# Two expert layers around attention on one core: token transposes ahead of their waits, layer-norm moments between the router's mask steps, the token table written in halves

## The chip, the cores and the metric

One core of one Trainium2 chip runs the whole program. The metric is the device time of one execution in microseconds. TensorE does matrix products and transposes, VectorE, ScalarE and GpSimd (POOL in the views) do the elementwise work, SyncE (SP) issues most DMAs. Each engine runs its own instructions in order; semaphores tie them together.

## The reference

The input x is 8 x 256 tokens of 256 numbers, fp32. Three residual layers follow each other:

```python
x = x + 0.5 * ffn(layernorm(x), router_w, w1, v1, w2)
x = x + attention(layernorm(x), Wq, bq, Wk, bk, Wv, bv, Wo, bo)
x = x + 0.5 * ffn(layernorm(x), router_w, w1, v1, w2)
```

`ffn` is a mixture of 64 experts of width 96. The eight highest of softmax(x @ router_w.T) are a token's experts, their weights are scaled to sum 1, an expert takes its first 32 tokens in an order that goes over the tokens, computes silu(x w1) * (x v1) and multiplies by w2; the weighted results are added back to the tokens. Attention has 16 heads of 128 in 4 groups that share keys and values, over 8 sequences of 256.

## The kernel before, in words

Tokens lie in 16 tiles of 128. Both expert layers run through the same helpers, named `expert_layer(layer)` on each engine, with attention between them.

**Router.** A pair of tiles is transposed on TensorE (`transpose_tokens`, L1178) and copied by ScalarE (`copy_tokens`, L556). `experts_of(n)` multiplies four tiles by the router's weights (L1188), ScalarE copies (L560), `logits_of(n)` transposes back (L1199), ScalarE copies to `logits` (L564). VectorE has a mask step for each four tiles: MAX8 (L822), MATCH_REPLACE8 of the eight highest (L826), and `chosen` by comparison (L828). GpSimd subtracts the maximum (L486), multiplies by 1/sigma (L490), ScalarE takes the exponential (L600), GpSimd multiplies by the mask (L494). The layer norm's statistics are BATCH_NORM_STATS2 (L742 at the start, L1020 behind attention), its moments a chain of small operations on VectorE (`moment_steps`, 11 levels at L755; `shifts`, L785). In layer 0 all 16 tiles go in one chain ahead of the masks; in layer 1 it is 12 tiles, and then the last four once attention has given them.

**Slots.** From `chosen` TensorE makes codes (L1226), VectorE finds each expert's tokens (L835 to L862, `slot_index`), ScalarE normalises the tokens (L574), and SP writes tokens (`store_tokens`, L379) and weights (`store_weights`, L385) to a table in HBM. When slots are known and the table is whole, GpSimd gathers 128 rows of it for each of 16 groups of four experts (L506). TensorE is kept busy with filler products meanwhile (`keep_busy`, L1121).

**Experts.** `slot_step(s)` of each engine handles one group: transpose of the slots (L1084), products with `up` (L1152), silu (L543) and product (L809), transpose (L1145) and copy (`hiddenT`, L539), products with `down` (L1162), and later the sums into tokens (L1113, L1097).

**Loads.** SP issues everything in one order. A group's weights are `up` (768 KB) and `down` (512 KB), into one of 12 homes named q, r, o, s. SP issues groups 0 to 3, the table, groups 4 to 11, then 12 to 15 as homes become free, with wk behind 12 and wv behind 13, wq and wo at the end. In layer 1 groups 0 to 3 are issued within attention, 4 to 7 at `attention_done`, then the table, and the others after the first two gathers.

**Attention weights.** fp32 values are split in a high and a low part: `split_high` on ScalarE (L622), `split_low` on VectorE (L931), in the order of the list `splits`. Four early ones stand in slot steps 11 to 15, the others in attention. `project` on TensorE waits until K_SPLIT, V_SPLIT or Q_SPLIT of them are done. `first_fills` is the order of the first projections: xT, xT, k, q, q, v, v, q, q; `in_fill` says behind which of them VectorE does a split.

## Time and profile before

| what | value |
|---|---|
| median of 3 runs | 687.88 us (687.8 to 689.42) |
| profiled execution, its own time | 689.65 us |
| its span, first to last instruction | 687.9 us |
| mean granted TensorE clock | 0.964 |
| TensorE busy | 630.9 us (92%) |
| VectorE busy | 504.6 us (73%) |
| ScalarE busy | 390.5 us (57%) |
| GpSimd busy | 50.8 us (7%) |

Times in the rows are from the start of the span. PE is TensorE, DVE is VectorE, ACT is ScalarE, SPq the queue in which SP issues DMAs, PEclk the granted clock as a share of 2.4 GHz. In a row `[2.25 <-DVE wq_lo L931]` says that the engine stood idle for 2.25 us before it and what ended that. A group such as "4.03 ACT L574 ... x8" is eight instructions that took 4.03 us from first start to last end.

### The profile page before, as it was taken

How to read it: one execution, taken by the hardware profiler on the slowest of the kernel's cores; microseconds unless marked ns; L12 is line 12 of the kernel's file. 1: busy time of each engine (PE TensorE's matmuls, PEld its weight loads, DVE VectorE, ACT ScalarE, POOL GpSimd, SP SyncE). 2: the span in 40 equal slices, each digit the busy share in tenths (PEclk: the TensorE clock that was granted, in tenths of full speed). 3: DMA queues.
4: the chain of work that ended last, by engine and by line, in shares of the span. 5: the costliest groups of instructions: out<-in, count | busy, mean ns of one | idle time of the engine just before them, and what ended most of it. 6: DMA issues, size and time to landing. Idle time of an engine off the chain costs nothing.

```text
span 687.9 us, 12266 instructions
## 1 busy us (share of the span) xinstructions
PE 630.9 (92%) x4626; PEld 542.3 (79%) x4626; DVE 504.6 (73%) x1312; ACT 390.5 (57%) x1051; POOL 50.8 (7%) x68
## 2 busy tenths in 40 slices
PE   8489887999999999999999999999999999947995
PEld 6267665899898979999897999989799998625774
DVE  5846656689997777778777777877777787684663
ACT  4724454567666565666655566665556666572341
POOL 2343000000000000000000000000000000034310
PEclk9779998899999999999999999999999999978998
DMA  9799960000000000000000000000000007196971
GB/s 316 259 386 403 373 221 1 0 1 1 1 2 1 1 0 1 1 1 1 1 1 1 1 0 1 1 1 1 1 1 1 1 7 301 70 369 242 344 271 49
DMA packets 27135, 62.53 MB, mean 91 GB/s; under 512 B 6880, under 2 KB 17120, under 8 KB 26816
## 3 DMA queue, kind: packets, MB, share of 16 engines
q1 hardware_dynamic: 25008, 55.92, 22.1%
q0 software_dynamic: 1632, 5.38, 2.2%
q8 instruction: 39, 0.64, 0.4%
q10 hardware_dynamic: 432, 0.39, 0.2%
q14 instruction: 24, 0.20, 0.1%
HBM read 54.34 MB, written 7.34 MB: 90 GB/s over the span
## 4 chain that ended last, share of the span: by engine, by line
PE 77%; DVE 9%; ACT 5%; DMA 3%; another core or an unknown queue 2%; issue 1%; POOL 1%; SPq 1%; DVEq 0%; POOLq 0%; ACTq 0%
PE bank L1291 19%; PE bank L1293 18%; PE bank L1292 18%; PE bank L1345 8%; PE bank L1113 3%; PE bank L1152 3%; DMA down_r<-down_in 3%; PE bank L1162 2%; PE bank L1084 1%; PE bank L1097 1%; PE bank L1266 1%; DMA slots<-token_table,slot_index 1%; DVE ln L755 1%; DVE o_lo L983 1%
## 5 line engine op out<-in xcount | busy, mean ns | idle before, releaser
L664 ACT ACTIVATE probs<-bank,negmax 128x256 f32<-128x256 f32 x256 | 121.5, 494 | 0.0
L677 ACT CAST probsT_hi<-bank 128x512 fp32r<-128x512 f32 x128 | 68.9, 590 | 82.3 <-PE bank L1345 82.3
L997 DVE TENSOR_REDUCE negmax<-bank 128x2 f32<-128x512 f32 x128 | 82.0, 681 | 2.3 <-PE bank L1293 2.3
L1029 DVE TENSOR_TENSOR probsT_lo<-bank,probsT_hi 128x512 fp32r<-128x512 f32 x128 | 82.0, 682 | 1.4 <-ACT probsT_hi L677 1.4
L647 ACT ACTIVATE o_hi<-bank,bv 128x512 fp32r<-128x512 f32 x64 | 44.2, 690 | 64.5 <-PE bank L1293 64.5
L1291 PE MATMUL bank<-k_hi,q_hi 128*128 128x256 f32 x256 | 73.2, 286 | 2.9 <-DVE q_lo L983 2.9
L1005 DVE TENSOR_SCALAR probs<-probs,rowinv 128x256 f32<-128x256 f32 x256 | 73.1, 350 | 2.3
L983 DVE SCALAR_TENSOR_TENSOR o_lo<-bank,bv,o_hi 128x512 fp32r<-128x512 f32 x64 | 48.0, 750 | 36.0 <-ACT o_hi L647 35.8
L1291 PE MATMUL bank<-o_hi,wo_hi 128*128 128x256 f32 x256 | 72.9, 285 | 0.7 <-DVE o_lo L983 0.7
L1293 PE MATMUL bank<-k_hi,q_lo 128*128 128x256 f32 x256 | 73.0, 285 | 0.0
L1292 PE MATMUL bank<-k_lo,q_hi 128*128 128x256 f32 x256 | 72.9, 285 | 0.0
L1293 PE MATMUL bank<-o_hi,wo_lo 128*128 128x256 f32 x256 | 72.3, 282 | 0.0
L1292 PE MATMUL bank<-o_lo,wo_hi 128*128 128x256 f32 x256 | 72.1, 282 | 0.0
L983 DVE SCALAR_TENSOR_TENSOR q_lo<-bank,bq,q_hi 128x512 fp32r<-128x512 f32 x64 | 48.0, 749 | 31.3 <-ACT q_hi L647 31.2
L1345 PE MATMUL bank<-ident,probs 128*128 128x128 f32 x512 | 67.2, 275 | 0.6 <-DVE probs L1005 0.6
L1345 PEld LDWEIGHTS bank<-ident,probs 128*128 128x128 f32 x512 | 58.2, 142 | 1.1 <-DVE probs L1005 1.1
L664 ACT ACTIVATION_READ_ACCUMULATOR probs<-bank,negmax 128x1 f32 x256 | 57.7, 225 | 0.0
L1291 PE MATMUL bank<-xT_hi,wq_hi 128*128 128x512 f32 x128 | 55.1, 430 | 2.3 <-DVE wq_lo L931 2.3
L1291 PE MATMUL bank<-probsT_hi,v_hi 128*128 128x512 f32 x128 | 51.4, 401 | 4.0 <-DVE xT_lo L981 3.2
L647 ACT ACTIVATE q_hi<-bank,bq 128x512 fp32r<-128x512 f32 x64 | 45.0, 702 | 17.1 <-PE bank L1293 17.1
L1291 PEld LDWEIGHTS bank<-k_hi,q_hi 128*128 128x128 f32 x256 | 49.4, 193 | 6.1 <-DVE q_lo L983 3.7
L1292 PEld LDWEIGHTS bank<-k_lo,q_hi 128*128 128x128 f32 x256 | 49.4, 193 | 2.3
(178 smaller groups left out, 1347.9 us busy)
## 6 DMA issues: line engine op xcount, KB each, us to landing
up_r<-up_in SPq DMA_DIRECT2D x16, 768.0 KB
down_r<-down_in SPq DMA_DIRECT2D x14, 512.0 KB
up_q<-up_in SPq DMA_DIRECT2D x8, 768.0 KB, 9.1
up_o<-up_in SPq DMA_DIRECT2D x6, 768.0 KB
down_q<-down_in SPq DMA_DIRECT2D x8, 512.0 KB, 10.1
token_table<-xn SPq DMA_DIRECT2D x16, 256.0 KB, 2.8
down_o<-down_in SPq DMA_DIRECT2D x6, 512.0 KB
x<-x_in SPq DMA_DIRECT2D x4, 512.0 KB, 5.6
```

The costliest lines, as they stand in the source:

```text
L647: nc.scalar.activation(dst, src, ACT.Identity, bias=bias).then_inc(work_high, 1)
L664: nc.scalar.activation(probs[:, n % 2, t, :], scores_ps[head][:, qt * S:qt * S + S], ACT.Exp, bias=negmax[:, n % 2, t:t + 1], accum_out=ro ...
L677: nc.scalar.copy(probsT[0][:, head].rearrange("p c s -> p (c s)"), probsT_ps[head][:]).then_inc(probsT_high, 1)
L983: nc.vector.scalar_tensor_tensor(lo, src, bias, hi.bitcast(f32), ALU.add, ALU.subtract).then_inc(work_taken, 1)
L997: nc.vector.reduce_max(negmax[:, n % 2, 2 * head:2 * head + 2], scores_ps[head][:].rearrange("p (t s) -> p t s", t=2), AX.X, negate=True). ...
L1005: last = nc.vector.tensor_scalar(probs[:, n % 2, t, :], probs[:, n % 2, t, :], rowinv[:, n % 2, t:t + 1], None, ALU.mult)
L1029: nc.vector.tensor_tensor(probsT[1][:, head].rearrange("p c s -> p (c s)"), probsT_ps[head][:], probsT[0][:, head].rearrange("p c s -> p ( ...
L1113: last = mm(banks[n][:, D * pair:D * pair + D], marks[:, c:c + P], parts, start=start and pair == 0, stop=stop, skip_group_check=True)
L1291: mm(dst, w[0], m[0], start=start, stop=False, skip_group_check=shared)
L1292: mm(dst, w[0], m[1], start=False, stop=False, skip_group_check=shared)
L1293: return mm(dst, w[1], m[0], start=False, stop=stop, skip_group_check=shared)
L1345: last = nc.tensor.transpose(probsT_ps[head][:, c * S + qt * P:c * S + qt * P + P], probs[:, n % 2, 2 * head + qt, c * P:c * P + P], ident[:])
```

## The change

- **Start.** 5 instead of 14 filler products. The first four tiles are transposed before the wait for the centred router weights, with other orders of transposes, expert products and logits in both layers; logits go through banks 2 and 3 instead of 6 and 7.
- **Moments.** A new `masks(layer, n, between)` on VectorE runs moment levels between its own operations. In layer 0 masks 0 and 1 hold all 11 levels. In layer 1 mask 0 with the levels of the first 12 tiles is done before the last output, and the moments of the last four tiles are on GpSimd (`last_moments`, 21 operations).
- **End of attention.** Tokens 0 and 1 of layer 1 are transposed in attention's last step; expert product 0, transposes 2 and 3 and logits 0 go before its last output product, expert product 1 and transposes 4 and 5 before its output transposes. `attention_done` is given before the last statistics.
- **Table.** GpSimd waits for all masks before it multiplies, then multiplies in two halves; exponentials and weights go in halves too. ScalarE normalises 12 tiles, takes the exponentials, then 4. SP writes tokens 0 to 2, weights 0, tokens 3, weights 1.
- **Loads.** Three groups instead of four before the table in layer 0, and two instead of four between `attention_done` and the table in layer 1. wk, the first quarter of wq, wv, the rest of wq and wo follow behind all groups.
- **Splits.** The first two of wq come before those of wv; all four early ones move out of steps 11 to 15 to the end of the first expert layer.

```diff
-            for g in range(4):
+            for g in range(3):
                 load(0, g)
-            for n in range(4):
-                store_tokens(n)
-            store_weights()
-            for g in range(4, AHEAD):
+            store_table()
+            for g in range(3, AHEAD):
                 load(0, g)
...
+            sp.dma_start(wq_raw[:, :, 0:G * DH], by_column[:, :, 0:G * DH]).then_inc(wq_first_loaded, 16)
...
-            for g in range(len(homes_q), 8):
+            for g in range(len(homes_q), 6):
                 load(1, g)
...
-        K_SPLIT, V_SPLIT, Q_SPLIT, O_SPLIT = 2, 4, [6, 8, 12, 16], [10, 14, 18, 20]
+        K_SPLIT, V_SPLIT, Q_SPLIT, O_SPLIT = 2, 6, [4, 8, 12, 16], [10, 14, 18, 20]
...
+            def store_table():
+                for n in range(3):
+                    store_tokens(n)
+                store_weights(0)
+                store_tokens(3)
+                store_weights(1)
...
+            def last_moments():
...
+                pool.wait_ge(last_stats, 1)
+                tt(half_gap, stats[:, a:b, 1], stats[:, a:b, 4], ALU.subtract)
+                tt(mean_, stats[:, a:b, 1], stats[:, a:b, 4], ALU.add)
+                tie(tt(var, stats[:, a:b, 2], stats[:, a:b, 5], ALU.add))
...
+                tie(tt(var, var, gap2, ALU.add))
+                tie(ts(rstd_.bitcast(i32), var.bitcast(i32), -0.5, ROOT_BITS, ALU.mult, ALU.add))
...
                 pool.wait_ge(shifted, shift_seen.add(4))
+                pool.wait_ge(chosen_ready, masks.add(4))
                 pool.wait_ge(moments_ready, 2 * layer + 1)
-                nc.gpsimd.tensor_tensor(expw[:], expw[:], rstd.unsqueeze(2).to_broadcast([P, TILES, E]),
-                                        ALU.mult).then_inc(scaled_ready, 1)
+                for h in range(2):
+                    tiles = slice(8 * h, 8 * h + 8)
+                    nc.gpsimd.tensor_tensor(expw[:, tiles, :], expw[:, tiles, :], rstd[:, tiles].unsqueeze(2).to_broadcast([P, 8, E]),
+                                            ALU.mult).then_inc(scaled_ready, 1)
...
+                if layer == 0 and s == GROUPS - 1:
+                    split_high(0)
...
-                normalise(0, TILES // 2)
+                normalise(0, TILES - 4)
...
             expert_layer(0)
+            for n in range(2, 5):
+                split_high(n)
...
+            def masks(layer, n, between=()):
...
+                for a in range(4 * n, 4 * n + 4):
+                    top = nc.vector.max(top8[:, a, :], logits[:, a, :])
+                    if a == 4 * n + 3:
+                        top.then_inc(top8_ready, 1)
+                    chore()
...
-            moments(0, TILES)
+            steps = moment_steps(0, TILES)
+            masks(0, 0, steps[:7])
+            masks(0, 1, steps[7:])
             shifts(0, TILES)
+            masks(0, 2)
+            masks(0, 3)
...
-            in_fill = {1: 4, 2: 5, 3: 6, 4: 7, 6: 8, 7: 9}
+            in_fill = {1: 3, 2: 4, 3: 5, 4: 6, 6: 7, 7: 8, 8: 9}
...
-            moments(0, TILES - 4)
+            masks(1, 0, moment_steps(0, TILES - 4))
             shifts(0, TILES - 4)
-            last = output(BLOCKS - 1)
-            nc.vector.sem_inc(attention_done, 1)
-            tie(last)
-            moments(TILES - 4, TILES)
-            shifts(TILES - 4, TILES)
+            output(BLOCKS - 1).then_inc(last_stats, 1)
+            for n in range(1, 4):
+                masks(1, n)
             expert_layer(1)
...
-            for _ in range(14):
+            for _ in range(5):
                 mm(bank[3][:, 0:P], ones, ones, start=True, stop=True)
...
-            for u in range(2):
-                transpose_tokens(1, u)
-            output_product(STEPS - 1)
             experts_of(1, 0)
             transpose_tokens(1, 2)
+            transpose_tokens(1, 3)
+            logits_of(1, 0)
+            output_product(STEPS - 1)
+            experts_of(1, 1)
+            transpose_tokens(1, 4)
+            transpose_tokens(1, 5)
             output()
             expert_layer(1)
```

## Rows read from the trace of the kernel before

**Rows 1.** Busy time by stage: us, busy (instructions) of each engine, clock, DMA, GB/s.
```profile
8.00:26.00 18.00, 10.99 (x78) 7.17 (x79) 16.66 (x85) 11.76 (x25) 4.39 (x5) 0.95 0.95 359
45.00:94.00 49.00, 44.91 (x562) 31.57 (x551) 31.03 (x116) 22.03 (x68) 9.65 (x11) 0.97 1.03 386
128.00:590.00 462.00, 453.54 (x2960) 408.83 (x2959) 368.82 (x786) 289.32 (x798) 0.00 (x0) 1.00 0.03 12
```

**Rows 2.** The chain that ended last, first router: start us, us, what.
```profile
15.30 0.19 DVE ln L755
20.14 0.53 DVE top L822 x4
...
21.59 0.42 DVE chosen L828
23.47 2.03 DVE chosen L828
```

**Rows 3.** Instructions in order of time, 1 to 26 us; x's landing; a small iota.
```profile
1.07 6.34 PE L1266 MATMUL bank<-xnT 128*128 128x128 f32 x28 [1.07 <-DVE xnT L726]
8.12 5.32 DVE L742 BATCH_NORM_STATS2 stats<-x 128x6 f32<-128x256 f32 x16
8.30 1.06 PE L1178 MATMUL bank<-ident,x 128*128 128x128 f32 x8 [0.49 <-issue]
22.61 0.62 POOL L486 TENSOR_TENSOR expw<-logits,top 128x256 f32<-128x256 f32 x1 [1.26 <-DVE top L822]
23.31 1.90 POOL L490 TENSOR_TENSOR expw<-expw,ln 128x1024 f32<-128x1024 f32 x1
...
DMA to landing us min/median/max: 4.1/5.6/7.3
...
L462 POOL IOTA part_offset<- 64x4 int32 x2 | 0.3, 131 | 0.1
```

**Rows 4.** Instructions in order of time, 20 to 33 us, ScalarE and SP's queue.
```profile
20.20 4.04 ACT L574 ACTIVATE xn<-x,ln 128x256 f32<-128x256 f32 x8
...
32.61 0.91 SPq L370 DMA_DIRECT2D up_r<-up_in  x1
```

**Rows 5.** End of the first expert stage: ScalarE in order of time, then the chain.
```profile
74.60 0.63 ACT L622 ACTIVATE wk_hi<-wk_raw 128x512 fp32r<-128x512 f32 x1 [2.90 <-DMA wk_raw<-wk_in]
...
69.98 17.71 DMA down_r<-down_in
```

**Rows 6.** Landing of wo; TensorE in order of time; the chain there.
```profile
DMA to landing us min/median/max: 21.8/21.8/21.8
...
105.66 0.47 PE L1291 MATMUL bank<-xT_hi,wq_hi 128*128 128x512 f32 x1 [2.25 <-DVE wq_lo L931]
...
107.60 0.43 PE bank L1293
```

**Rows 7.** TensorE, the last output product, in order of time.
```profile
592.28 0.39 PE L1291 MATMUL bank<-o_hi,wo_hi 128*128 128x256 f32 x1 [0.69 <-DVE o_lo L983]
```

**Rows 8.** The second router, in order of time.
```profile
596.06 1.28 DVE L1014 TENSOR_TENSOR x<-x,bank 128x512 f32<-128x512 f32 x2 [1.15 <-PE bank L1371]
608.90 2.02 DVE L828 TENSOR_TENSOR chosen<-struck,logits 128x256 fp32r<-128x256 f32 x1
611.64 4.04 ACT L574 ACTIVATE xn<-x,ln 128x256 f32<-128x256 f32 x8
```

**Rows 9.** From slots to the experts of layer 1, in order of time.
```profile
621.58 5.51 PE L1121 MATMUL bank<-router_w,ident 128*128 128x128 f32 x32
622.24 1.00 POOL L506 DMA_INDIRECT slots<-token_table,slot_index  x1 [8.07 <-DVE slot_index L862]
625.21 0.22 DVE L794 TENSOR_REDUCE total<-slots 128x1 f32<-128x64 f32 x1 [2.83 <-DMA slots<-token_table,slot_index]
629.30 0.37 ACT L605 COPY slotsT<-bank 128x256 f32<-128x256 f32 x1 [12.11 <-remote]
630.09 0.86 PE L1152 MATMUL bank<-up_q,slotsT 128*32 128x192 f32 x16
```

More of the change, by code:

```diff
@@ L483, in expert_layer @@
                 for n in range(4):
+                    if layer == 1 and n == 1:
+                        last_moments()
                     pool.wait_ge(top8_ready, tops.add())
@@ L534, in slot_step @@
                                    bank[0][:, 0:KD * P]).then_inc(slotsT_ready, 1)
-                if layer == 0 and SPLIT_AT <= s < SPLIT_AT + SPLIT_EARLY:
-                    split_high(s - SPLIT_AT)
                 if s > 0:
@@ L540, in slot_step @@
                                    bank[2][0:F, 0:P]).then_inc(hiddenT_ready, 1)
+                if layer == 0 and s == GROUPS:
+                    split_high(1)
                 if s < GROUPS:
@@ L679, in step @@
                 jobs = fills(n, last)
+                if last and n == STEPS - 1:
+                    copy_tokens(0)
+                    copy_tokens(1)
                 for head in range(2):
@@ L810, in slot_step @@
                                             ALU.mult).then_inc(hidden_ready, 1)
+                if layer == 0 and s == GROUPS:
+                    split_low(0)
+                    split_low(1)
                 if s > 0:
@@ L1381, in step @@
                 jobs = fills(n, last)
+                if last and n == STEPS - 1:
+                    for u in range(2):
+                        transpose_tokens(1, u)
                 for m, job in enumerate(jobs):
```

192 lines of the change are left out of this document (118 added, 74 removed).

## The prediction

> **What bounds the kernel now.** I read the busy time by stage first [rows 1]. From 128 to 590 us TensorE is busy 453.5 of 462 us at full clock: that is attention, and the change leaves it alone. The rest, some 225 us, is two expert layers with a router ahead of each. In 8 to 26 us VectorE is the busy one (16.7 of 18 us), and layer 1's router is built like this one; in 45 to 94 us the DMA engines never rest (share 1.03, 386 GB/s); between routers and experts runs a chain of short steps.
>
> The second view is the chain that ended last. In the first router it is VectorE without a break: the moments, then four mask steps of 1.88 us each (from the maxima at 20.14 to the end of `chosen` at 22.01), and the last mask's final operation takes 2.03 us instead of 0.42 [rows 2]. It starts 0.16 us after a GpSimd multiply of 1.90 us and ends 0.3 us after it [rows 3]: two engines in each other's way, 1.6 us lost. The same stands in layer 1 (2.02 us at 608.90) [rows 8].
>
> Third, the SP queue. It issues four loads, then stands until tokens and weights of the table are ready, since its order has them first, and issues the next load only at 32.61 [rows 4]. All later loads hang on that time, and the chain of the first expert stage ends on the load of the last group, which lands at 87.69 us [rows 5].
>
> **Sum for layer 0.** Today 14 first matmuls (28 records) run from 1.07 to 7.41, 0.226 us each, and column sums, centring and only then the statistics (8.12) follow [rows 3]. With 5 of them TensorE is through at 3.4. The x pieces are issued from 1.23 to about 2.8 and take 4.1 to 7.3 us, so they land from 5.3 to 10.1 [rows 3]. The last four statistics (0.33 us each) end at 11.4 instead of 13.44: 2.0 us gained.
>
> The clock takes part of it back. 0.226 us for a record is half clock (1.2 GHz); the same 128-column transposes take 0.13 us at full clock, after 6 us of activity [rows 3]. The 9 matmuls taken away were that activity. The new first token transposes start at 5.3, probably at half clock. Two pairs of transposes, one expert product and one transpose of logits, 1.1 + 0.6 + 1.1 + 0.4 us and copies at full clock, take some 7 us at half: logits 0 are there at about 12.3, logits 1 at about 15.8. VectorE then does a mask (1.88) and seven moment levels. A level alone costs 0.20 us [rows 2]; between maxima I take 0.15, since the wait for its predecessor is filled. The GpSimd subtraction of 0.62 us runs at that time and can block the levels that read two tiles, as it blocked the mask [rows 3]; I take 0.3 us (0 to 0.6). So masks 0 and 1 with all moments end at 18.3, the shift at 18.5, masks 2 and 3 at 22.3, against 25.50: 3.2 us, of which 1.6 is the collision, since the multiply now waits for the last mask.
>
> ScalarE begins to normalise at 18.6 instead of 20.20. Twelve tiles at 0.505 us (4.04 for 8) reach 24.6, two half exponentials 25.7, four tiles 27.7 [rows 4]. SP issues tokens 3 and the second half of the weights by 30.0. The loads resume there instead of 32.61. But only three loads were issued ahead instead of four. From 32.61 to 87.69 twelve groups and wk and wv (0.8 of a group) landed, 4.3 us for one [rows 4 and 5]. Now thirteen groups come first, and the attention weights behind: 30.0 + 13 x 4.3 = 85.9 instead of 87.69. **Gain 1.8 us**, and its point of no gain is a restart at 31.8. The gathers go off 3.4 us sooner, but that is hidden by these loads. The wait of ScalarE for wk at 74.6 (2.90 us idle) goes [rows 5], but the load takes its place.
>
> Behind the last group wk, the first quarter of wq and wv must land at about +1.5, +3.0 and +4.5 us after it. ScalarE asks for them, in order, at +1.9, +4.1 and +5.3 us (its positions in steps 15 and 16); behind the first of these waits stands its copy of hiddenT, for which TensorE waits. Priced at nothing, at most 1.5 us. ScalarE has one split between the copies of x and its table load now, where it had two: **0.5 us**. wo, issued at 76.5, took 21.8 us to 98.3 [rows 6] and comes 0.6 us after ScalarE wants it; k_hi is 2.6 us away, so nothing.
>
> **Head of attention.** TensorE waits 2.25 us for wq_lo, because q needs six splits and VectorE does the last behind k; then it runs at half clock (0.43 us start to start for 512 columns instead of 0.23) for ten matmuls [rows 6]. With q ahead of wv in the order of splits q needs four, done in the fill before. I follow the fills with that: scores start 6.7 us after xT instead of 10.1. v now needs split 6 and costs a bit. I take **3.0 us**, ends 1.0 and 4.0 (the wait alone less the new one for v, or all of the half clock as well).
>
> **Layer 1.** Tokens 0 and 1 are transposed (1.03 us) ahead of an output product, so the last attention product comes 0.85 us later. TensorE then does an expert product, two pairs of transposes and a transpose of logits before the last output product, 2.5 us where 1.0 us of work and 0.69 of waiting stood [rows 7]. Output of x is done at about 599.45 instead of 597.34: 2.1 us later. Mask 0 with 11 levels of moments (about 3.9 us) lies ahead of it on VectorE, from 594.05, and ends about when y comes; its old cover was idle time. After it VectorE has 1.4 us of statistics and three masks without moments: 600.85 + 3 x 1.88 + 0.3 us of blocking = 606.8 against 610.92 [rows 8]. Everything up to the slots follows, and the 16 filler products start at 617.5 instead of 621.58. They take 5.5 us to 623.0, and the first gather (3.0 us from issue to VectorE's first use) lands at 621.2, so they stay last [rows 9]. **4.1 us.**
>
> The table must keep up. Counting row times through the new order, ScalarE has its last logits at 603.6, the identity copies till 604.5, 12 tiles till 610.6, exponentials till 611.7, the last tiles till 613.7 (615.68 now); weights issued by 615.4 land at about 618, when slots are ready too [rows 8]. GpSimd: attention_done at 599.5, two operations, one subtraction, 601.0; then 21 small operations, 17 of them in a chain. The trace has none like these there. Lower bound: 0.131 us (a 4-element iota) with 0.08 between, 4.4 us. Upper: 0.62 (a 256-element one), 15 us. The two tensor_tensor sizes, 0.62 for 256 and 1.90 for 1024 elements, give 0.19 plus 1.67 ns for each element [rows 3]; I take 0.20 and 0.12 us between: 6.0 us, to 607.0. Three subtractions, two multiplies: 611.0, and ScalarE comes to the exponentials at 610.6. So 0.3 us is lost, hidden by 0.7 us of slack ahead of SP's turn.
>
> The Trainium skill, "GPSIMD Engine Reference", section 4.1, says the opposite of the change: elementwise work belongs on VectorE, GpSimd being about twice as slow with two inputs. Rows here give 0.62 against 0.42 us for 256 elements. By its factor on the 2.75 us of moments the sum would be 5.5 us and no other.
>
> Loads: two groups instead of four ahead of the table, so it meets less traffic; groups 6 to 11 then start at about 623. Group 6 is wanted 16 us after the start of the experts, group 11 32 us; at 4.3 us a group they are in time.
>
> Between the end of the fillers (627.1) and ScalarE's copy of slot 0 (629.30, released by "remote") lie 0.2 us for two transposes and some 2.0 us for which the trace names nothing [rows 9]. I can't say whether they stay: half of it, **1.0 us** (0 to 2).
>
> Sum: 1.8 + 0.5 + 3.0 + 4.1 + 1.0 = 10.4 us. The profiled execution took 689.65 us around a span of 687.9, so 679.2; the median of the three runs is 687.88, so **677.5 us**.
>
> **Rivals.**
> (a) *The loads eat layer 0.* If the restart is later than 31.8, one group fewer ahead costs up to 4.3 - 2.6 us. For: half clock in the first router. With no gain there and 1.5 us of waits for wk: 677.5 + 1.8 + 1.5 = 680.8. Chance 0.17.
> (b) *The new wait takes the gain of layer 1.* GpSimd's chain at 0.4 us an operation plus gaps is 10.5 us: the end of the table slips 4 us, and with it the gathers: 681.5. Chance 0.10.
> (c) *Slower than before.* The same chain at 1.00 us each, the time of this engine's gather instruction [rows 9]: 22 us with less between, gathers 16 us later than in my sum less 0.7 of slack, 692.8. It passes the time of before from about 0.72 us an operation. Against: every arithmetic row of this engine lies on the line above. Chance 0.03.
> (d) *It doesn't do what it says*: TensorE's early work only delays the end of attention and logits come as late as before, the layer 1 part is nil: 682.6. Against: three of four masks need no late logits. Chance 0.06.
> (e) *All covers hold*: clock up early, full 4.0 at the head, 2.0 us gone: 687.88 - (3.4 + 0.5 + 4.0 + 4.1 + 2.0) = 673.9. Chance 0.14.
> Forecast, 675 to 680: 0.50.
>
> Range 672.5 to 683: it takes in (a), (b), (d) and (e). About 0.3% (2 us) is what a measurement of this kernel can tell. Faster by more: 0.92; within 0.03; slower 0.05 ((c), and part of what I haven't seen).
>
> **What would show it.** Layer 0: statistics end near 11.4; the last chosen is 0.42 us long and ends near 22.3; first up_r issue near 30 and last load near 86; no wait at TensorE for wq_lo. Layer 1: x added 2 us later, last chosen near 607, GpSimd's chain about 6 us, no long wait of a gather for the table, experts 5 us sooner. Wrong if the half clock reaches past 12 us, if GpSimd's operations are far above 0.2 us, or if the waits for wk, wq or wv stop ScalarE at the end of the first expert stage.

## The result and the profile after

| what | before | after |
|---|---|---|
| median beside each other | 688.1 us (687.8 to 689.42, 4 runs) | 678.81 us (677.92 to 681.17, 4 runs) |
| profiled execution, its span | 689.65, 687.9 us | 678.44, 676.7 us |
| mean granted clock | 0.964 | 0.973 |
| from the start to the addition of x in layer 1 | 596.06 | 590.16 |
| from there to the first `up` of layer 1 | 34.03 | 27.88 |
| from there to the end of the span | 57.8 | 58.66 |

The changed kernel takes 0.9867 of the time before (95% interval 0.9838 to 0.9895); a second series gave 0.9865 (0.9842 to 0.9888). The difference is 9.3 us between medians and 11.2 us between the spans of the two profiled runs: that of before lies 1.55 us above its median, that of after 0.37 below. The last three lines of the table split the 11.2 us: 5.9 and 6.15 gained, 0.85 lost.

Line numbers are new: the moments are L813, `chosen` L896, `best_rank` L913, `part_bits` L915, the gather L544, `up` L1228, the fillers L1197. The same stretches as in [rows 1], with the same columns:

```profile
8.00:26.00 18.00, 14.38 (x86) 8.44 (x84) 15.78 (x88) 14.11 (x31) 6.12 (x8) 0.81 0.87 321
45.00:94.00 49.00, 43.68 (x523) 32.43 (x517) 29.94 (x116) 22.87 (x65) 8.47 (x9) 0.97 1.03 385
128.00:590.00 462.00, 453.65 (x2982) 409.07 (x2981) 367.18 (x803) 290.38 (x799) 0.00 (x0) 1.00 0.03 12
```

TensorE is busy for 14.38 of the 18 us at clock 0.81, where it was for 10.99 at 0.95; 3.68 us of the 14.38 are products on tokens that came behind 26 us before. VectorE is no longer the one that never rests there (15.78 against 16.66). The loads run at 385 GB/s as before, and attention is the same.

The first router of after, answering to [rows 2, 3], in order of time (start us, length us, engine, line, operation, and in brackets the idle time before it):

```profile
9.98 1.40 DVE L800 BATCH_NORM_STATS2 stats<-x 128x6 f32<-128x256 f32 x4 [0.32 <-DMA x<-x_in]
...
12.66 0.62 POOL L522 TENSOR_TENSOR expw<-logits,top 128x256 f32<-128x256 f32 x1 [6.71 <-DVE top L886]
...
12.81 0.50 DVE L813 TENSOR_TENSOR ln<-ln 128x16 f32<-128x16 f32 x1
...
20.09 0.43 DVE L896 TENSOR_TENSOR chosen<-struck,logits 128x256 fp32r<-128x256 f32 x1
...
24.41 2.49 POOL L533 TENSOR_TENSOR expw<-expw,chosen 128x512 f32<-128x512 f32 x2 [1.71 <-ACT expw L652]
...
26.12 0.82 DVE L913 CAST best_rank<-best 128x32 int32<-128x32 f32 x1
```

The statistics end at 11.38, and what ends VectorE's wait is the landing of x. One level of moments takes 0.50 us instead of 0.16, and a subtraction of GpSimd runs beside it. The last `chosen` takes 0.43 us, where it took 2.03 [rows 2]. But `best_rank`, 0.18 us long in other runs, takes 0.82 beside the mask multiplication, which now comes at that time.

Loads and the head of attention in after, answering to [rows 4 to 6]:

```profile
28.95 0.57 SPq L371 DMA_DIRECT2D up_q<-up_in  x1
...
83.32 1.15 PE L1228 MATMUL bank<-up_r,slotsT 128*32 128x192 f32 x16 [2.27 <-DMA down_r<-down_in]
...
104.46 0.47 PE L1375 MATMUL bank<-wv_hi,xT_hi 128*128 128x512 f32 x1 [0.40 <-DVE wv_lo L1003]
...
105.91 0.28 PE L1375 MATMUL bank<-k_hi,q_hi 128*128 128x256 f32 x1
...
118.41 0.47 PE L1375 MATMUL bank<-xT_hi,wk_hi 128*128 128x512 f32 x1
```

SP issues loads again at 28.95 (32.61 before), and the load of the last group ends TensorE's wait at 83.27 (87.69). The wait of 2.25 us for wq_lo is gone; one of 0.40 us for wv_lo stands in its place. The scores start at 105.91.

The second router of after, answering to [rows 8]:

```profile
590.16 1.28 DVE L1090 TENSOR_TENSOR x<-x,bank 128x512 f32<-128x512 f32 x2
...
592.97 0.20 POOL L488 TENSOR_TENSOR ln<-stats 128x4 f32<-128x4 f32 x1 [0.86 <-DVE stats L1098]
...
598.09 0.42 DVE L896 TENSOR_TENSOR chosen<-struck,logits 128x256 fp32r<-128x256 f32 x1
...
598.20 0.37 POOL L506 TENSOR_TENSOR ln<-ln 128x4 f32<-128x4 f32 x1
...
598.94 0.23 POOL L508 TENSOR_SCALAR ln<-ln 128x4 f32<-128x4 f32 x1
...
603.25 2.52 POOL L533 TENSOR_TENSOR expw<-expw,chosen 128x512 f32<-128x512 f32 x2 [0.21 <-ACT expw L652]
...
603.68 0.88 DVE L913 CAST best_rank<-best 128x32 int32<-128x32 f32 x1
...
604.68 1.24 DVE L915 TENSOR_TENSOR part_bits<-best_code,bit_of_part 128x128 int32<-128x128 int32 x1
```

GpSimd's chain runs from 592.97 to 599.17. The last `chosen` ends at 598.51 and is short. Again the collision has moved: `best_rank` takes 0.88 and `part_bits` 1.24 us beside the two mask multiplications (2.52 us), 1.65 us more than the 0.18 and 0.29 that they take where nothing runs beside them. It works the other way round too: of GpSimd's 21 small operations three take 0.35 to 0.37 us where their like take 0.20, and each of the three begins within a `chosen` of VectorE and ends 0.05 to 0.07 us after it (the row at 598.20).

From the slots to the experts of layer 1, answering to [rows 9]:

```profile
610.38 6.61 PE L1197 MATMUL bank<-router_w,ident 128*128 128x128 f32 x32
...
611.05 1.07 POOL L544 DMA_INDIRECT slots<-token_table,slot_index  x1 [5.28 <-DVE slot_index L933]
...
616.58 0.94 POOL L544 DMA_INDIRECT slots<-token_table,slot_index  x1 [0.30 <-issue]
...
618.04 0.86 PE L1228 MATMUL bank<-up_q,slotsT 128*32 128x192 f32 x16
...
623.56 0.41 PE L1160 MATMUL bank<-ident,slots 128*128 128x128 f32 x2 [0.56 <-DMA slots<-token_table,slot_index]
```

The fillers take 6.61 us (5.51 before). The gather issued at 616.58 lands at 623.4, 6.8 us later, and TensorE waits 0.56 us for it.

### The profile page after: what moved, and what is told of

It reads as the page before. It is cut to its first block, busy times and chain, and to the rows that moved or that the text cites. A ratio compares the mean times of both kernels' runs of the same rounds, so it can differ in the third digit from the quotient of the medians.

```text
span 676.7 us, 12242 instructions
## 1 busy us (share of the span) xinstructions
PE 625.8 (92%) x4608; PEld 538.1 (80%) x4608; DVE 500.7 (74%) x1297; ACT 390.5 (58%) x1053; POOL 56.1 (8%) x93
## 3 DMA queue, kind: packets, MB, share of 16 engines
q0 software_dynamic: 1632, 5.38, 2.2%
## 4 chain that ended last, share of the span: by engine, by line
PE 74%; DVE 11%; DMA 7%; ACT 3%; issue 2%; POOL 1%; SPq 0%; DVEq 0%; ACTq 0%; POOLq 0%
PE bank L1375 19%; PE bank L1377 18%; PE bank L1376 18%; PE bank L1429 8%; PE bank L1189 3%; DMA down_r<-down_in 3%; DMA slots<-token_table,slot_index 3%; PE bank L1228 2%; PE bank L1238 1%; PE bank L1173 1%; DMA x<-x_in 1%; DVE struck L892 1%; PE bank L1160 1%; DVE ln L813 1%; ACT probs L717 1%
## 5 line engine op out<-in xcount | busy, mean ns | idle before, releaser
L700 ACT ACTIVATE o_hi<-bank,bv 128x512 fp32r<-128x512 f32 x64 | 44.2, 690 | 63.7 <-PE bank L1377 63.7
## 6 DMA issues: line engine op xcount, KB each, us to landing
up_r<-up_in SPq DMA_DIRECT2D x16, 768.0 KB, 12.3
```

The costliest lines, as they stand in the source:

```text
L700: nc.scalar.activation(dst, src, ACT.Identity, bias=bias).then_inc(work_high, 1)
```

## Experiments

Each is compared with the kernel before on the same chip; run N below is the one under number N. The changed kernel itself, in its second series, is the measure for the small differences (an "x us more" is between its median and the run's). Runs 1 to 3 stood beside it on one chip; 4 to 7 were taken on a second chip, 8, 9 and 11 on a third, 10 in a later series on the first. The kernel before had 688.13, 688.16, 687.14 and 687.25 us in these four series, so a difference across them is uncertain by about 1 us, and the ratios to the kernel before are the better measure:

> The changed kernel itself, so that the experiments beside it have it on the same chip. It had 0.9867 of the kernel before (0.9838 to 0.9895). Expected: the same within 0.3%, about 679 us where the kernel before has 688; last chosen of layer 0 at 20.5 us of the span, first up of layer 1 at 618.0. If the first comparison had owed part of its 9.3 us to the chip, the ratio would come out above 0.99.

Measured: 679.35 us (677.09 to 681.18, 6 runs), 0.9865. Its rows repeat the first trace: last `chosen` at 20.54, `up` of layer 1 at 618.56. From the start of x's addition to that `up` it has 27.92 us (27.88). Single runs of one kernel spread over 4 us, so below the rows decide wherever medians lie within 2 us.

**1. Moments back on VectorE.**

```diff
-                    if layer == 1 and n == 1:
-                        last_moments()
...
-            output(BLOCKS - 1).then_inc(last_stats, 1)
+            tie(output(BLOCKS - 1))
+            moments(TILES - 4, TILES)
+            shifts(TILES - 4, TILES)
```

> The moments of the last four tiles of layer 1 go back from GpSimd to VectorE; all else is the changed kernel. Theory (VectorE is the path in layer 1's router, from the x addition to the last chosen): its 24 small instructions return to a chain that costs about 0.13 us for each, 24 x 0.13 = 3.1 us, so the last chosen ends about 3 us later than at 598.5 and the kernel takes about 681.7 us (+2.9). Rival (the slot fillers and the first gather set the start of layer 1's experts, and VectorE's last chosen has slack): within 0.5 us of the changed kernel. A second rival, GpSimd's chain was itself late at the end (last level 599.2 after a last chosen that ended at 598.5): then taking it away costs only about 2 us.

Measured: 681.28 us, 0.9892 (0.9874 to 0.991), 1.9 us more. VectorE in order of time:

```profile
608.46 0.18 DVE L911 CAST best_rank<-best 128x32 int32<-128x32 f32 x1
...
608.75 0.29 DVE L913 TENSOR_TENSOR part_bits<-best_code,bit_of_part 128x128 int32<-128x128 int32 x1
```

The last `chosen` ends 11.1 us after x's addition started, 8.35 in the changed kernel: 2.7 us, as the theory says. But the masks come later than GpSimd's multiplications (604.99 to 607.50) now, `best_rank` and `part_bits` are back at 0.18 and 0.29, and 1.2 us come back: `up` starts 29.11 us after x's addition, against 27.88. Moving the moments brought 2.7 us on VectorE and gave 1.2 back in a collision of its own making (and 0.3 in fillers that ran longer at half clock). Between medians the part is not clear of the spread: the intervals of the two ratios overlap.

**2. v before q.**

```diff
+            sp.dma_start(wv_raw[:], wv_in.rearrange("(k p) n -> p k n", p=P)).then_inc(wv_loaded, 16)
             sp.dma_start(wq_raw[:, :, 0:G * DH], by_column[:, :, 0:G * DH]).then_inc(wq_first_loaded, 16)
-            sp.dma_start(wv_raw[:], wv_in.rearrange("(k p) n -> p k n", p=P)).then_inc(wv_loaded, 16)
...
-        K_SPLIT, V_SPLIT, Q_SPLIT, O_SPLIT = 2, 6, [4, 8, 12, 16], [10, 14, 18, 20]
+        K_SPLIT, V_SPLIT, Q_SPLIT, O_SPLIT = 2, 4, [6, 8, 12, 16], [10, 14, 18, 20]
...
-            in_fill = {1: 3, 2: 4, 3: 5, 4: 6, 6: 7, 7: 8, 8: 9}
+            in_fill = {1: 4, 2: 5, 3: 6, 4: 7, 6: 8, 7: 9}
```

> The head of layer 0's attention back as it was: v's weights are loaded and split before the first q's, with the places of the split in the order of the projections moved back; all else is the changed kernel. Theory: of the changed kernel's gain, 3.3 us (loads to last slot transposes to scores) and 1.3 us (second and third projections at full instead of half clock) came from q being computed before v, so this takes 3.3 to 4.6 us more than the changed kernel, about 682.5 us, and VectorE's low half of the first q's weights is again what the tensor engine waits for near 103 us. Rival: the head follows the loads of the last expert group alone, and the order of q and v moves nothing; within 0.5 us of the changed kernel.

Measured: 680.75 us, 0.9896 (0.9867 to 0.9925), 1.4 us more.

```profile
103.87 0.47 PE L1376 MATMUL bank<-xT_hi,wq_hi 128*128 128x512 f32 x1 [2.25 <-DVE wq_lo L1003]
...
117.29 0.39 PE L1376 MATMUL bank<-k_hi,q_hi 128*128 128x256 f32 x1 [2.68 <-DVE q_lo L1059]
```

The wait for wq_lo is back to the hundredth. From the last wait for weights (83.95) to the second block's first scores (117.29) it takes 33.3 us; 31.3 and 31.5 in the two traces of the changed kernel. The order is worth 1.9 us here, not the 3.3 to 4.6 expected. The rest of what the head gained is clock, which can fall either way: these scores run at full clock (0.39 us), those of the changed kernel at half (0.58). So at a later landmark, the second block's first product for v, little of the 1.9 us is left: it comes 38.92 us after the last wait, 38.34 and 38.63 in the two traces of the changed kernel.

**3. Fourteen fillers.**

```diff
-            for _ in range(5):
+            for _ in range(14):
```

> Fourteen pairs of filler products ahead of layer 0's router instead of five; all else is the changed kernel. Theory (the early router is on the path to the restart of the weight loads): the logits start about 2 us later than at 11.0 us if the fillers hold the tensor engine, the last chosen of layer 0 ends about 1.5 to 2 us later than at 20.5, the loads restart so much later than at 28.95, and the kernel takes about 680.6 us (+1.8). Rival 1 (the landing of x at 10.0 us holds the statistics whatever the tensor engine does, and the fillers end before it): within 0.3 us. Rival 2 (the fillers bring the clock up earlier): the logits at full clock, 0.5 us faster.

Measured: 680.08 us, 0.9883 (0.9862 to 0.9904), 0.7 us more, which is inside the spread. The statistics wait for the centred weights again and run from 7.12 to 12.43, so the last `chosen` of layer 0 ends at 21.54, 1.0 us later, yet the loads restart at 29.09 against 28.95. Five traces of other kernels whose code is the changed kernel's up to there (its second series, runs 1, 2, 4 and 5) restart them at 28.02 to 29.90. Taking the fillers away gave VectorE 1 us and the loads nothing that can be measured.

**4. Four groups ahead of the table in layer 1**, as before the change:

```diff
-            for g in range(len(homes_q), 6):
+            for g in range(len(homes_q), 8):
...
-            for g in range(6, AHEAD):
+            for g in range(8, AHEAD):
```

> Four expert groups of weights instead of two are issued ahead of the table's stores in layer 1, as in the kernel before; all else is the changed kernel. Theory (the loads of layer 1 compete with the gathers: the gather issued at 616.6 took 6.8 us while loads that were issued from 615.4 ran): with two groups loaded earlier the gathers meet fewer loads, and the wait of 0.56 us and the late hidden near 620 go, 0.3 to 1.0 us less. Rival (the table stands behind the two groups on its queue, 2 groups by some 4 us): the table is stored later, the first gather lands later than 614.07 and, beyond 3 us, the experts of layer 1 start later; 0 to 3 us slower.

Measured: 683.53 us, 0.9942 (0.9921 to 0.9963), 4.2 us more. GpSimd and TensorE:

```profile
614.37 1.07 POOL L544 DMA_INDIRECT slots<-token_table,slot_index  x1 [9.60 <-issue]
...
617.46 0.44 PE L1160 MATMUL bank<-ident,slots 128*128 128x128 f32 x2 [1.44 <-DMA slots<-token_table,slot_index]
```

The first gather starts at 614.37, though x was added 1.0 us sooner than in the changed kernel, whose gather starts at 611.05. Its wait is not ended by slot_index but by the table ("issue": no event of an engine). The stores of tokens into the table take 7.2 us to land in the median (2.4 in the changed kernel, 4.5 in the kernel before). So the rival holds. The edit of two numbers, which I had priced at nothing, is worth 4.2 of the 9.3 us (5.3 us by the ratios, whose intervals lie apart).

**5. Eight fillers in layer 1.**

```diff
-                keep_busy(16)
+                keep_busy(8 if layer == 1 else 16)
```

> Eight pairs of filler products instead of sixteen between slot keys and slot transposes of layer 1; all else is the changed kernel. Theory (in the changed kernel the fillers end at 617.0, 2.9 us after the first gather landed at 614.07, so that they and not the gather set the start of layer 1's experts): they end near 613.7, the first slot transposes start at the gather's landing, near 614.1 instead of 616.8, and the kernel takes 1 to 2.7 us less, about 677 us; less where fewer fillers leave the clock low at the start of the experts. Rival (the weights of the first groups or slotsT hold the experts anyway): within 0.5 us of 679.35, the changed kernel's median beside the first experiments.

Measured: 680.85 us, 0.9892 (0.9873 to 0.9911), 1.5 us more.

```profile
617.16 0.86 PE L1228 MATMUL bank<-up_q,slotsT 128*32 128x192 f32 x16
...
622.88 0.66 PE L1160 MATMUL bank<-ident,slots 128*128 128x128 f32 x2 [2.67 <-DMA slots<-token_table,slot_index]
...
623.68 1.51 PE L1228 MATMUL bank<-up_q,slotsT 128*32 128x192 f32 x16
```

The experts do start 2.3 us sooner after x's addition (25.58 against 27.88). Then TensorE waits 2.67 us for the third group's tokens, and the next `up` takes 1.51 us instead of 0.86: half clock. From that `up` to the end it takes 63.7 us instead of 58.7. The gain that was expected is not there: the next limit is the gathers. The 1.5 us between medians are not clear of the spread.

**6. Masks in pieces.**

```diff
-                    nc.gpsimd.tensor_tensor(expw[:, 8 * h:8 * h + 8, :], expw[:, 8 * h:8 * h + 8, :],
-                                            chosen[:, :, h, :].bitcast(f32), ALU.mult).then_inc(weights_ready, 1)
+                    for part in range(4):
+                        a = 8 * h + 2 * part
+                        last = nc.gpsimd.tensor_tensor(expw[:, a:a + 2, :], expw[:, a:a + 2, :],
+                                                       chosen[:, 2 * part:2 * part + 2, h, :].bitcast(f32), ALU.mult)
+                    last.then_inc(weights_ready, 1)
```

> GpSimd's multiplication of the exponentials by the masks, two instructions of 2.5 us in each layer, is issued in four pieces each; all else is the changed kernel. Theory (VectorE's instructions wait while a GpSimd instruction runs, so best_rank takes 0.88 instead of 0.18 and part_bits 1.24 instead of 0.29 in layer 1, 1.65 us together, and best_rank 0.82 in layer 0): a blocked instruction waits for one piece of about 0.7 us at most, so part_bits takes under 0.9 us, the slot keys of layer 1 are ready 0.3 to 1.0 us sooner after the last chosen (11.6 us in the changed kernel), and the kernel takes 0.3 to 1.0 us less, or nothing less if the fillers behind the slot keys take it up. Rival (the time goes with the bytes both engines move, not with the length of GpSimd's instruction): the two instructions are as long as before. Cost: 6 more GpSimd instructions per layer, by 0.1 to 0.2 us, and the table up to 1 us later.

Measured: 680.71 us, 0.9892 (0.9873 to 0.9911), 1.4 us more.

```profile
605.66 0.48 DVE L916 CAST best_rank<-best 128x32 int32<-128x32 f32 x1
...
606.26 0.43 DVE L918 TENSOR_TENSOR part_bits<-best_code,bit_of_part 128x128 int32<-128x128 int32 x1
...
605.23 3.57 POOL L535 TENSOR_TENSOR expw<-expw,chosen 128x128 f32<-128x128 f32 x8 [0.21 <-ACT expw L655]
...
613.46 1.07 POOL L547 DMA_INDIRECT slots<-token_table,slot_index  x1 [4.66 <-issue]
```

`best_rank` and `part_bits` take 0.48 and 0.43 us now, so VectorE waits for the end of the instruction that is running, not for bytes. But eight pieces take 3.57 us instead of 2.52, and the first gather waits for the table, no longer for slot_index. The cost has moved to the table, and behind it TensorE waits 2.57 us for the third group's tokens (0.56 in the changed kernel): `up` comes 1.84 us sooner after x's addition (26.04 against 27.88), and from there to the end it takes 61.9 us instead of 58.7. In layer 0 SP waits for the eight pieces too: in this trace loads restart at 30.31 and the last wait for weights ends at 85.43, later than in any trace of the changed kernel's layer 0 (82.5 to 84.0), and x is added at 592.14 instead of 590.16.

**7. Four groups ahead in layer 0.**

```diff
-            for g in range(3):
+            for g in range(4):
                 load(0, g)
             store_table()
-            for g in range(3, AHEAD):
+            for g in range(4, AHEAD):
```

> Four expert groups of weights instead of three are issued ahead of the stores of the token table in layer 0; all else is the changed kernel. Theory (the loads are the path in layer 0, one group in 4.2 us, and they stand still between the landing of the first loads and the restart at 28.95): part of the still stand is filled, the last group lands up to 3 us sooner than at 83.3, the kernel takes 1 to 3 us less. Rival (the queues never stand still, or the table's stores are held up behind the fourth group as long as it takes): the last group lands within 0.3 us of 83.3, or the first gathers and the first up are later, and the kernel is 0 to 2 us slower.

Measured: **674.59 us**, 0.9806 (0.9782 to 0.9831), 4.8 us less than the changed kernel. The trace, of a run of 676.17 us, shows half of it:

```profile
81.14 0.86 PE L1228 MATMUL bank<-up_r,slotsT 128*32 128x192 f32 x16 [1.72 <-DMA down_r<-down_in]
...
619.53 0.41 PE L1160 MATMUL bank<-ident,slots 128*128 128x128 f32 x2 [1.62 <-DMA slots<-token_table,slot_index]
```

The last wait for weights ends at 81.14 instead of 83.32 and is 1.72 us long, although the loads restart at 30.08, 1.1 us later. Nothing of the table suffers: the first gather waits for slot_index. x is added 2.0 us sooner (588.16). In layer 1 this trace shows a wait of 1.62 us for tokens. The intervals of the two ratios lie apart.

**8. Five groups ahead.** The same two lines with 5.

> Five expert groups of weights issued ahead of the stores of the token table in layer 0; all else is the changed kernel, which has three. Four gave 674.6 us (0.9806 of the kernel before), with the last wait for weights at 81.14 instead of 83.32 us. Theory (each group ahead takes its time from the stage that waits for the last load, until no wait is left): of the last wait, 1.72 us with four, nothing is left, the stage ends up to 1.7 us sooner, and the kernel takes 673 to 674.6 us. Rival (the fifth group is in the air when the table is stored and the tokens are gathered, as in layer 1, where two more groups ahead cost 4.2 us): the first gather or the first group's tokens come later, and the kernel is 0 to 3 us slower than with four.

Measured: 676.1 us, 0.9839 (0.9825 to 0.9854), 1.5 us more than with four, 2.3 us by the ratios, whose intervals just overlap.

```profile
35.24 1.11 POOL L544 DMA_INDIRECT slots<-token_table,slot_index  x1 [8.06 <-issue]
...
41.41 0.44 PE L1160 MATMUL bank<-ident,slots 128*128 128x128 f32 x2 [3.49 <-DMA slots<-token_table,slot_index]
```

No wait for weights is left in layer 0. In its place the first gather waits for the table (8.06 us idle, "issue") and goes off at 35.24 (33.59 with four), and TensorE waits 3.49 us for tokens (0.43 with four). One wait has been put in the place of the other. Five groups are no better than four; that they are worse is likely, but not shown clear of the spread.

**9. Loads behind four gathers**, on top of 7:

```diff
             def wait_for_gathers(layer):
-                for n in range(2):
+                for n in range(4):
```

> The kernel with four groups ahead in layer 0, and in layer 1 the loads behind the table start after the fourth gather has landed instead of the second. Theory (in layer 1 a gather that is issued once the loads run takes 6 us and more to land instead of 3, so TensorE waits for the tokens of the third to fifth group: 1.62 us at 619.5 with four ahead, 2.67 us at 622.9 with fewer fillers): the wait of 1.62 us goes or falls under 0.5 us, the loads start about 2.5 us later, which the experts do not notice (group 6 is wanted 16 us after their start), and the kernel takes 1 to 1.6 us less than with four ahead alone, about 673.3 us. Rival (the third gather waits for nothing but its own engine, or the later gathers meet the loads all the same): within 0.5 us of 674.6, with the wait at a later group.

Measured: **671.84 us**, 0.9775 (0.976 to 0.9789). DMA issues of the changed kernel from 604 to 630 us (count, then median us to landing), and then of this kernel from 604 to 620:

```profile
slots<-token_table,slot_index POOLq DMA_INDIRECT x10, 6.5
```

```profile
slots<-token_table,slot_index POOLq DMA_INDIRECT x9, 3.0
...
611.52 0.86 PE L1228 MATMUL bank<-up_q,slotsT 128*32 128x192 f32 x16
```

The gathers issued up to 620 us land in 3.0 us instead of 6.5 (up to 630 us it is twelve gathers with a median of 4.6: the later ones still meet loads), and TensorE waits nowhere over 0.35 us for tokens. From the first `up` to the end it has 58.0 us (59.5 in 7). That is 1.5 us, as expected, of the 2.8 between the medians (2.1 by the ratios). The two traces differ by 4.9 us, 3.2 of them ahead of x's addition, in stretches that this edit does not touch: this trace has its last wait in layer 0 at 1.24 us and the clock stays up, that of run 7 has 1.72 us there and it falls. So part of the gap between runs 7 and 9 is chance.

**10. The same with eight fillers in layer 1.**

> The best kernel so far (four groups ahead in layer 0, loads of layer 1 behind the fourth gather; 671.84 us) with eight pairs of filler products instead of sixteen in layer 1. On the changed kernel the same edit made it slower (680.85 us against 679.35): the experts started 2.3 us sooner after the addition of x, then TensorE waited 2.67 us for the tokens of the third group and worked 5 us at half clock. Theory (that wait came from the gathers that met the loads, and it alone ate the gain): now no gather meets loads before 612.7 of 669.5 us, so the experts start up to 1.6 us sooner, when the first tokens have landed (608.9 in the best kernel, where the fillers end at 610.5), and the kernel takes 0.8 to 1.6 us less, about 670.6 us. Rival (fewer fillers leave the clock at its lower level at the start of the experts, or the gathers follow each other by 1.26 us and the third is late however free the queues are): a half clock longer by 2 us or a new wait at the third group, 672 us or more.

Measured: **670.85 us**, 0.9773 (0.9744 to 0.9802), the lowest median, though the ratio is that of 9 (0.9775).

```profile
611.12 0.41 PE L1160 MATMUL bank<-ident,slots 128*128 128x128 f32 x2 [0.89 <-DMA slots<-token_table,slot_index]
```

TensorE waits 0.89 us for the first tokens, and `up` comes 25.62 us after x's addition (26.60 in 9), at full clock; no later wait is over 0.35 us. From `up` to the end it takes 58.4 us (58.0 in 9), so 0.5 us is left of the gain on the rows, and by the ratios nothing. In 5 the stretch behind `up` lost 5.1 us to late gathers; here that loss is gone, as the theory had it, but that the kernel gets faster by this edit is not shown.

**11. The kernel before with one wait moved.**

```diff
+                pool.wait_ge(chosen_ready, masks.add(4))
                 pool.wait_ge(moments_ready, 2 * layer + 1)
...
                 pool.wait_ge(exps, exp_seen.add())
-                pool.wait_ge(chosen_ready, masks.add(4))
```

> The kernel before, with one edit of the change: GpSimd waits for all masks before it multiplies by 1/sigma, instead of after. Theory (the two collisions, chosen at 2.03 and 2.02 us instead of 0.42, are caused by that multiplication): chosen takes 0.42 us in both layers. Layer 1 gains 1.6 us less what the later multiplication costs; in layer 0 the slots are ready 1.6 us sooner, but the loads hold the stage, so 0 to 0.4 us: 686 to 686.5 us. Rival (the collision only moves, since the multiplication of 1.90 and the one of 2.36 us now run beside the steps that find the slots): best_rank and part_bits become 0.7 and 1 us longer and half or more of the gain is given back, 687.3 us or more. It also shows whether the 2.0 us ahead of the first slotsT of layer 1, which no row explained, recur when the routers end sooner.

Measured: 690.55 us (684.41 to 694.21, 12 runs), 1.0033 (1.0006 to 1.0059): 0.1 to 0.6% slower than the kernel before by its interval, where the theory expected 686 to 686.5 us. The trace is of a run of 693.29 us.

```profile
609.94 0.42 DVE L828 TENSOR_TENSOR chosen<-struck,logits 128x256 fp32r<-128x256 f32 x1
...
623.61 0.99 POOL L506 DMA_INDIRECT slots<-token_table,slot_index  x1 [7.66 <-issue]
...
633.35 0.41 PE L1084 MATMUL bank<-ident,slots 128*128 128x128 f32 x2 [2.09 <-DMA slots<-token_table,slot_index]
...
636.29 0.66 PE L1084 MATMUL bank<-ident,slots 128*128 128x128 f32 x2 [1.03 <-DMA slots<-token_table,slot_index]
```

Both last `chosen` take 0.42 us, so the cause of the collision is right, and `best_rank` and `part_bits` keep their 0.18 and 0.29, so it has not moved. Yet nothing is left of it in the time. In layer 0 the exponentials come 0.5 us later and SP's loads restart at 33.07 (32.61 in [rows 4]). The last wait for weights ends at the same time, 87.7, but is 2.16 us long instead of 0.98, the clock falls behind it, and x is added 1.0 us later (597.10). In layer 1 the table is now what the first gather waits for (623.61 against 622.24 in [rows 9]). `up` still starts 31.1 us after x's addition instead of 34.0, but then waits of 2.09 and 1.03 us for tokens and half clock follow, and the experts take 63.3 us instead of 57.8. Neither theory had it. That `best_rank` was not met has a reason in the rows: the multiplication now runs beside the two operations on `keys` that read a bank of TensorE's results, and these don't wait (last section). What this edit gains in the changed kernel, with the table in halves and fewer loads ahead of it, was not measured.

No run takes out TensorE's early work at the end of attention, mask 0 ahead of the last output, the table in halves, or the loads of wk, wq and wv behind all groups. What these brought is read from the rows of before and after alone.

## Why the prediction came out as it did

The forecast of 677.5 us stands against a median of 678.81 us; its sum, 10.4 us, against 11.2 us on the two spans and 9.3 us between medians. Its steps, one by one:

**Early router of layer 0: right in kind, too small.** Statistics ended at 11.38 (forecast 11.4). The blocked level cost 0.34 us (0.3). But half clock reached less far than I had it: the first logits were there at 11.0, not 12.3. (That this was half clock rests on lengths: twelve transposes take 2.94 us from 5.38, eight take 1.06 at 8.30 in the kernel before. The granted clock of both traces stands at 1.00 in every window up to 14 us.) And a level between maxima costs next to nothing: a mask step with four levels took 2.13 us, those without any 1.97 (with a shift) and 1.89, so about 0.06 us a level instead of 0.15. The last `chosen` ended at 20.52 instead of 22.3.

**Loads: 4.4 us instead of 1.8**, the forecast's term furthest off. The restart came at 28.95, 1.05 us before my 30.0. The pace made the rest: 13 groups in 54.3 us, 4.18 for one, where I had divided a stretch with wk and wv in it and had 4.3. Of the rival that the loads eat layer 0 the mechanism was right: one group fewer ahead costs 2.2 us at the last wait and 4.8 between medians, as run 7 shows. But the earlier restart paid for it. Chance has a share in both figures: in the six traces with this code up to there (the changed kernel twice, runs 1, 2, 4 and 5) loads restart at 28.02 to 29.90 and the last wait ends at 82.5 to 84.0, which puts the gain between 3.8 and 5.2 us.

**ScalarE's waits for wk, wq and wv: nothing**, as priced. **The head of attention, 3.5 us with the split: measured 2.9** from the last load to the second block's v (41.28 against 38.39 us). Within it, k came 1.85 us later after the last load (15.91 against 14.06), and from there on 4.74 us were gained. The longer wait for the last load (2.27 us against 0.98) is followed by half clock: 0.81 in 83 to 92 us, and `up` takes 1.15 us instead of 0.86. I had not asked what a longer wait does to the clock; the last section shows that it does so each time. Run 2 gives 1.9 us to the order of q and v itself, up to the scores of the second block. From these scores to v it took 8.34 us before, 7.03 after and 5.58 in run 2, and 5.58 and 7.12 in runs 9 and 10, whose code is the same up to there. So 1.3 of the 2.9 us come from a stretch that varies by 1.5 us by itself.

**x added 2.1 us later: 1.4.** The 7.3 us that attention came sooner became 5.9.

**Router of layer 1: right.** From the end of x's addition to the last `chosen` 13.58 us became 7.07; the steps of the prediction give 7.35. GpSimd's chain took 6.2 us (6.0): 0.20 us for most operations and 0.08 between, with three of 0.35 to 0.37, beside `chosen`. The rivals with 0.4 or 1.0 us an operation are out. Run 1 puts the net worth of moving the last moments at 1.2 us on the rows and 1.9 us between medians; the rest of this gain, mask 0 and TensorE's work ahead of the addition, was not taken out in any run.

**"Everything up to the slots follows": wrong.** From the last `chosen` to the slot fillers 10.66 us became 11.87. I had counted the collision that goes and not the one that comes: the masks are now multiplied beside `best_rank` and `part_bits`. A second loss stands behind it, the fillers at 6.61 us instead of 5.5, since the clock is 0.50 in 612 to 616 us. Together 2.3 us.

**The 2.0 us without a name: gone**, where I took half. Between the fillers' end and `up` 3.0 us became 1.05. Runs 2 and 3 show 1.9 and 2.0 us there, seven traces, the changed kernel's among them, 1.0 to 1.1. In run 11, the kernel before but for one wait, TensorE waits 0.78 us, for tokens. So it comes and goes in part without any edit there, and its cause stays open.

**"The table meets less traffic", priced at nothing: the step that I missed most.** Run 4 shows 4.2 us. Without this edit of the load order the table takes the place of the slots: `up` comes 2.35 us later after x's addition (30.23 against 27.88) and the experts take 1.6 us longer, so that of the 5.3 us that layer 1 gained net 1.3 would be left. It is the rival (b) with another cause: not a slow GpSimd, but stores that meet loads.

**Experts of layer 1: 0.85 us lost**, forecast nothing. I had asked whether weights come in time, and not tokens: the third group's came late by 0.56 us.

So the sum holds as 7.3 - 1.4 + 6.15 - 0.85 = 11.2, and the prediction was near it because mis-sized terms offset each other: +2.6 (loads) and +1.0 (no name) against -0.6 (head), -2.3 (slots and fillers), -0.85 (experts), and +0.7 and +0.3 from x's addition and the masks.

The rule of "GPSIMD Engine Reference" in the Trainium skill, section 4.1, that elementwise work belongs on VectorE, and that GpSimd is about twice as slow with two inputs, is not borne out for operations this small: 0.20 us against VectorE's 0.16 on 4 elements a partition (run 1). The move paid, since GpSimd was free. What did cost was the other thing: GpSimd's long instructions hold up VectorE's.

## What to carry to other kernels

When an edit makes a stage earlier, list what now runs beside it and what is next to be late, above all the small transfers behind large loads: the two largest effects that a single edit had here (4.2 and 4.8 us) were in the number of loads ahead of a table, not in the arithmetic. Count loads ahead until the wait for weights and the wait for tokens balance. And test a part alone on the old kernel as well as taken out of the new one: the wait that the new kernel has brought the old one nothing, though it did end the collision that it was meant to end.

## What the runs showed of the hardware

- Elementwise VectorE instructions that read and write SBUF alone (`chosen`, a moment level, `best_rank`, `part_bits`) do not run beside an elementwise one of GpSimd but last until its end: 0.42 us became 2.03, 0.16 became 0.50, 0.18 up to 1.15, 0.29 became 1.24. A small GpSimd operation that begins within `chosen` ends just after it, with 0.35 to 0.37 us instead of 0.20. MAX8 and MATCH_REPLACE8 don't wait: 0.43 and 0.41 us beside GpSimd's multiplications in run 1, as without. Nor do elementwise ones with an operand in a bank of TensorE's results: in the kernel before two of them take 0.42 us each in the midst of one GpSimd multiplication. The GpSimd multiplication and one of the two:

```profile
26.38 2.36 POOL L494 TENSOR_TENSOR expw<-expw,chosen 128x1024 f32<-128x1024 f32 x1 [1.17 <-DMA token_table<-xn]
...
27.23 0.42 DVE L836 TENSOR_TENSOR keys<-keys,bank 128x256 f32<-128x256 f32 x1
```

- A short VectorE operation that waits for its predecessor takes 0.20 us in a chain, and lengthens a mask step by 0.06 us when it stands between two maxima, by 0.09 between two replacements.
- A gather lands in 3.0 us on queues without loads (run 9) and in a median of 6.5 us where most meet loads (the changed kernel); the 256 KB stores of tokens in 2.4 us, and in 7.2 us behind two groups of loads more (run 4).
- TensorE's clock after its last wait for weights in layer 0. In the traces where that wait was 0 (run 8), 0.98 (before), 1.08 and 1.24 us (runs 10 and 9), k's first product came 14.0 to 14.1 us after it; where it was 1.72 (run 7) or 1.95 to 2.67 us (all others), 15.7 to 17.3 us after it, with the clock at its lower level for a part. The windows of run 8 and of the changed kernel, columns as in [rows 1]:

```profile
83.00:97.00 14.00, 11.87 (x108) 10.18 (x100) 9.96 (x31) 11.04 (x21) 0.00 (x0) 1.00 0.66 228
```

```profile
83.00:97.00 14.00, 12.06 (x102) 9.91 (x103) 7.56 (x26) 9.44 (x18) 0.00 (x0) 0.88 0.92 327
```

Run 7 and run 9 have the same code up to there, and the load lands at nearly the same time (81.1 and 81.4 us), but TensorE waits 1.72 us for it in one and 1.24 in the other, and k's product then comes 2.0 us later in run 7. All 14 traces fit this, but no run changes the length of this wait by itself, so that it is the wait which lowers the clock is argued from them.
